# Dense products of the first layer as three fp32r products of split operands, in a new order of steps

## The chip, the core and the metric

The kernel runs on one core of a Trainium2 chip. Its time is the device time of one execution in microseconds (us). The engines of the core are called PE (matmul; PEld is its weight load), ACT (ScalarE), DVE (VectorE), POOL (GpSimd) and SP (SyncE, which only issues transfers).

## What is computed

Two transformer layers in fp32. The change concerns the first, a cross attention with a feed-forward network, over 8 batches. x and the context are stored channels first, 256 channels by 512 tokens each; there are 16 heads of 16 channels. Cut to what matters, the first layer is

```python
q  = transpose(zt_prev + pos_enc, (0, 2, 1));  kv = transpose(za + pos_enc, (0, 2, 1))
q  = layer_norm(q, ln_q_g, ln_q_b);            kv = layer_norm(kv, ln_kv_g, ln_kv_b)
Q, K, V = split(q @ Wq), split(kv @ Wk), split(kv @ Wv)
attn = einsum('bhqd,bhkd->bhqk', Q, K) / sqrt(DH)
ctx  = einsum('bhqk,bhkd->bhqd', softmax(attn), V)
r    = ctx @ Wo + q
h    = layer_norm(r, ffn_ln_g, ffn_ln_b)
out  = gelu(h @ W1 + b1) @ W2 + b2 + r         # W1: 256x512, W2: 512x256
```

The second layer takes this output (8 x 256 x 512): self attention, cross attention and a network of 512 to 2048 to 512. It is in the functions `attention_layer` (tiles "b_...") and the network behind it ("c_...").

## The kernel before

`first_layer` (tiles "a_...") runs one program per engine. Time is counted in iterations i = -2, -1, 0, ... of 16 positions; each position has two half positions. In iteration i the softmax of batch i runs, the tail (output product, normalising, network) of batch i-1, and the head (input, normalising, queries, keys) of batches i+1 and i+2. The last two iterations (7 and 8) are interleaved with the start of the second layer.

In each half position PE computes one exponent pair E (`exp_scores`, L461-472: two matmuls of 128x512 into `escore`) and one maximum pair M (`max_scores`, L475-484, into `mscore`, 9 positions ahead of E). ACT takes the exponent of E (L639, 128x1024, into a ring `pt`), DVE the row maxima of M (L802, `row_maximum`, 128x1024). E, ACT's exponent and M, DVE's maximum each have one buffer, so the next E or M waits for the engine behind it. The maxima of a group of four heads are turned ("m"), made negative and split (L646, L837), and go through DRAM into the rows of the operand `qst`.

Between these pairs PE does the filler that the table `STEPS` lists by position; in it ("f1", -1, 2, 0) is step f1 of batch i-1, tile m=2, contraction piece k=0:
- "pv" (L499): values weighed by the exponents, 16 matmuls of 32x512 a half position; "ctx" (L508) and "ctxT" (L516) turn the result to tokens (there DVE divides it by the row sum, `divide_context`) and to channels again;
- "y" (`output`, L522), "f1" (`up`, L569), "f2" (`down`, L577), "q" and "k" (`project`, L553) are fp32 products of 128x512, one a step: 4 y, 8 f1, 8 f2, 4 q, 4 k per batch; "v" (`values`, L561) is eight of 128x256;
- "tok" (L537) turns an input or the residual to tokens, where DVE normalises it (statistics L810-815, `apply` L822, with the reciprocal root on POOL, L446); "chan" (L546) turns it back, and ACT adds gain and shift (L691).

These fillers share four PSUM banks in the order of `STEPS`; `claim` waits for the reader of the use four before. ACT, DVE, SP and POOL follow orders of their own, written out in their functions `position` (L733, L873) and `body` (L404, L449). In position 8 ACT does `gelu` (L720), with a load of another function table before and behind it. `high_part` (ACT, L699) and `low_part` (DVE, L830) split queries and keys into two fp32r parts for the score matmuls: the high part is the value written as fp32r, the low part the value less the high part. SP writes these parts to DRAM (`put`) and reads them back stacked (`stack`, L384, per group of four heads). `fetch` brings the inputs of batch i+3, to which POOL adds the positions (L440).

## Time and profile before

| | us |
|---|---|
| time, median of 3 runs | 1841.54 (1839.46 to 1841.65) |
| time of the profiled execution | 1842.27 |
| span of the profiled execution | 1840.5 |
| PE busy in the span | 1717.6 (93%) |
| DVE busy | 1207.0 (66%) |
| ACT busy | 1060.4 (58%) |
| POOL busy | 142.4 (8%) |
| granted clock of PE, mean | 0.959 |

The first layer takes roughly the first 770 us of the span, the second the rest. The trace gives records: an instruction's start, its duration, and the idle time before it with what ended it. Matmuls are pipelined, so a record is longer than the distance to the next; distances from start to start tell the pace. One record of the trace is half of an fp32 128x512 product: its two passes are recorded each for itself.

### The profile page before, as it was taken

Reading aid. Unit: us, or ns where it says so; the run is one execution under the profiler, and the core shown is the slowest. Engines: PE = TensorE matmul, PEld = TensorE weight load, DVE = VectorE, ACT = ScalarE, POOL = GpSimd, SP = SyncE. Lnnn points to the kernel's source line nnn. Section 1 sums busy time; section 2 is a strip of 40 time slices with the busy share of each in tenths; the row PEclk is TensorE's granted clock in tenths of the full one; section 3 lists DMA queues with packets and bytes.
Section 4 is the critical chain, followed back from the end, with each engine's and each line's share of the span. In section 5 each row is a group of like instructions: output and inputs, shape, how many; then the busy total and the mean of one; then the engine's idle time right before and its main releaser. Section 6 shows DMA issues by size and latency. Waiting matters only on the chain.

```text
span 1840.5 us, 32546 instructions
## 1 busy us (share of the span) xinstructions
PE 1717.6 (93%) x11840; PEld 1233.4 (67%) x11840; DVE 1207.0 (66%) x2792; ACT 1060.4 (58%) x2333; POOL 142.4 (8%) x207
## 2 busy tenths in 40 slices
PE   3879999999999988999999999999999899999999
PEld 2424343444434333788889888888888789999998
DVE  5666776767776552588888888888888663333332
ACT  2345666756666564587788777777777631111111
POOL 2110101101000000000000000100000100000000
PEclk8779999999999898999999989999999999999999
DMA  6322223222222222567557757666666330000000
GB/s 161 111 86 67 94 82 100 71 93 88 83 71 68 80 61 87 152 157 182 153 156 200 198 163 200 169 173 173 167 167 168 116 121 25 25 25 25 25 26 13
DMA packets 169479, 201.62 MB, mean 110 GB/s; under 512 B 25956, under 2 KB 117220, under 8 KB 169320
## 3 DMA queue, kind: packets, MB, share of 16 engines
q1 hardware_dynamic: 169032, 199.14, 38.5%
q8 instruction: 95, 1.56, 0.4%
q10 hardware_dynamic: 288, 0.39, 0.2%
q14 instruction: 64, 0.52, 0.1%
HBM read 131.84 MB, written 67.63 MB: 108 GB/s over the span
## 4 chain that ended last, share of the span: by engine, by line
PE 81%; DVE 9%; ACT 5%; issue 2%; DVEq 1%; DMA 1%; ACTq 0%; POOL 0%; SPq 0%
PE c_d L2121 10%; PE b_d L1379 10%; PE c_sums L2136 10%; PE b_d L1391 9%; PE a_d L499 6%; PE b_d L1458 5%; PE a_escore L472 5%; PE a_d L569 3%; PE a_d L577 3%; PE a_mscore L484 3%; PE a_d L553 3%; PE b_score L1446 3%; PE b_d L1475 3%; DVE a_mx L802 2%; PE a_d L561 2%
## 5 line engine op out<-in xcount | busy, mean ns | idle before, releaser
L802 DVE TENSOR_REDUCE a_mx<-a_mscore 128x2 f32<-128x1024 f32 x247 | 302.3, 1224 | 171.8 <-PE a_mscore L484 170.2
L639 ACT ACTIVATE a_pt<-a_escore 128x1024 f32<-128x1024 f32 x256 | 262.5, 1025 | 165.1 <-PE a_escore L472 164.9
L1605 ACT ACTIVATE b_pr<-b_t,b_nmax 128x256 f32<-128x256 f32 x512 | 254.5, 501 | 121.4 <-DVE b_nmax L1781 121.0
L2220 ACT ACTIVATE c_gT<-c_d,c_b 128x256 f32<-128x256 f32 x128 | 53.7, 472 | 267.4 <-PE c_d L2121 267.4
L1777 DVE TENSOR_TENSOR b_t<-b_score,b_mask 128x1024 f32<-128x1024 f32 x128 | 155.0, 1211 | 75.6 <-PE b_score L1446 75.6
L1781 DVE CUSTOM_DVE_ANT_0 b_t<-b_t,b_minus 128x256 f32<-128x256 f32 x512 | 191.1, 429 | 16.9
L472 PEld LDWEIGHTS a_escore<-a_qst,a_kst 50*128 50x128 f32 x512 | 50.0, 191 | 180.4 <-ACT a_pt L639 109.6
L472 PE MATMUL a_escore<-a_qst,a_kst 50*128 50x512 f32 x512 | 133.8, 518 | 24.2 <-ACT a_pt L639 23.7
L2265 DVE CAST c_g_high<-c_gT 128x512 fp32r<-128x512 f32 x64 | 38.1, 595 | 172.0 <-ACT c_gT L2220 172.0
L2121 PE MATMUL c_d<-c_ln_high,c_w_high 128*128 128x256 f32 x512 | 145.4, 284 | 2.4 <-DVE c_ln_low L2267 2.4
L2121 PE MATMUL c_d<-c_ln_high,c_w_low 128*128 128x256 f32 x512 | 145.6, 284 | 0.0
L2121 PE MATMUL c_d<-c_ln_low,c_w_high 128*128 128x256 f32 x512 | 145.6, 284 | 0.0
L1458 PE MATMUL b_d<-b_ident,b_pr 128*128 128x128 f32 x1024 | 136.8, 277 | 4.9 <-DVE b_xr L1819 2.5
L1617 ACT ACTIVATE b_pt<-b_d 128x512 f32<-128x512 f32 x256 | 137.2, 590 | 4.5 <-PE b_d L1458 3.4
L484 PE MATMUL a_mscore<-a_kst,a_qst 48*128 48x512 f32 x494 | 113.0, 451 | 24.2 <-DVE a_mx L802 13.5
L499 PE MATMUL a_d<-a_pt,a_vaug 128*32 128x512 f32 x1024 | 131.2, 633 | 0.0
L1458 PEld LDWEIGHTS b_d<-b_ident,b_pr 128*128 128x128 f32 x1024 | 117.6, 143 | 6.1 <-DVE b_kparts L1752 3.1
L1379 PE MATMUL b_d<-b_lnp,b_wq 128*128 128x256 f32 x768 | 106.3, 298 | 15.5 <-DVE b_encp L1735 14.7
L1379 PEld LDWEIGHTS b_d<-b_lnp,b_wq 128*128 128x128 f32 x768 | 100.4, 203 | 18.6 <-issue 18.6
L2136 PE MATMUL c_sums<-c_w_high,c_g_high 128*128 128x512 f32 x256 | 102.0, 398 | 7.5 <-issue 6.7
L2121 PEld LDWEIGHTS c_d<-c_ln_high,c_w_high 128*128 128x128 f32 x512 | 98.8, 193 | 4.5 <-issue 2.6
L2136 PE MATMUL c_sums<-c_w_high,c_g_low 128*128 128x512 f32 x256 | 100.4, 392 | 0.0
(166 smaller groups left out, 3255.5 us busy)
## 6 DMA issues: line engine op xcount, KB each, us to landing
b_qst<-b_q SPq DMA_DIRECT2D x96, 256.0 KB, 4.7
b_kst<-b_k SPq DMA_DIRECT2D x96, 256.0 KB, 6.4
b_q<-b_qparts SPq DMA_DIRECT2D x64, 256.0 KB, 4.5
b_k<-b_kparts SPq DMA_DIRECT2D x64, 256.0 KB, 3.6
a_qst<-a_q_parts SPq DMA_DIRECT2D x192, 64.0 KB, 2.2
a_kst<-a_k_parts SPq DMA_DIRECT2D x186, 64.0 KB, 2.2
...
```

The costliest lines, as they stand in the source:

```text
L472: mm = nc.tensor.matmul(escore[:, e, :], kst[rows, pair, k * P:(k + 1) * P], qst[rows, pair, :], start=True, stop=True)
L484: mm = nc.tensor.matmul(maxima_bank(b, n)[:, e, :], qst[rows, pair, q * P:(q + 1) * P], kst[rows, pair, :], start=True, stop=True)
L499: mm = nc.tensor.matmul(at[32 * j:32 * j + 32, :], vaug[:, k, GROUP * g + j, :], pt[:, (b * UNITS + pair * TT + k) % RING, e, :], start=(k ...
L639: nc.scalar.activation(pt[:, at % RING, :, :], escore[:], ACT.Exp, scale=SCALE).then_inc(exp_done.sem, 1)
L802: nc.vector.tensor_reduce(mx[:, 2 * pair:2 * pair + 2, q], maxima_bank(b, n)[:], AX_X, ALU.max).then_inc(max_done.sem, 1)
L1379: mm = nc.tensor.matmul(at[:, j * S:(j + 1) * S], w[:, x, k, m:m + P], src[:, y, k, :], start=(k == 0 and c == 0), stop=(k == KT - 1 and c ...
L1391: mm = nc.tensor.matmul(at, src[:, x, k, n * P:(n + 1) * P], w[:, y, k, :], start=(k == 0 and c == 0 and not biased), stop=(k == KT - 1 an ...
L1458: last = nc.tensor.transpose(at[:, j * P:(j + 1) * P], pr[:, u % 2, j, k * P:(k + 1) * P], ident[:])
L1605: last = nc.scalar.activation(pr[:, u % 2, j, :], t[:, u % 2, j, :], ACT.Exp, scale=-1.0, bias=nmax[:, u, j:j + 1], accum_out=esum[:, u, j ...
L1781: last = nc.vector.tensor_tensor_reduce(t[:, u % 2, j, :], t[:, u % 2, j, :], minus[s][:, q, :], -1.0, HUGE, ALU.add, ALU.min, accum_out=n ...
L2121: mm = nc.tensor.matmul(bank[:, j * S:(j + 1) * S], w1[w][:, k, m:m + P], lnp[v][:, k, :], start=(k == 0 and n == 0), stop=(k == KT - 1 an ...
L2136: mm = nc.tensor.matmul(sums[:, t_, :], gp[v][:, u % RING, at:at + P], w2[:, row, :], start=(k == 0 and n == 0), stop=(k == FT - 1 and n = ...
```

## The change

All dense products of the first layer are made of three fp32r matmuls: high weights with high activations, high weights with low, low weights with high. The weights are loaded raw into the ring `pt`, and split once, by ACT (`high_weight`) and DVE (`low_weight`). The activations are split in every batch: the attention's context by ACT and DVE straight out of PSUM (`context`, `low_context`), queries and hidden by a copy on ACT (`high_queries`, `high_hidden`) and a subtraction on DVE (`low_queries`, `low_hidden`), gelu's output in two halves (`high_gelu`, `low_gelu`), the normalised key and value input on POOL (`split_context`: a cast and a subtraction). One tile `pair` holds the split context, hidden, low gelu half and queries in turn (`pair_free` waits for the last reader). Tiles are shared more: `xin` also holds the tokens and the turned input (`room`, `tokens_of`), `tokr` also the hidden. `STEPS` and the orders of ACT, DVE, POOL and SP are new.

```diff
-        wo = sb("wo", [P, CT, C])
+        wo = sb("wo", [P, 2, CT, C], F32R)
...
+        PRODUCTS = ((0, 0), (0, 1), (1, 0))
...
-            9: [("k", 1, 1, 0), ("k", 1, 1, 1), ("q", 1, 1, 0), "E0", "M0", ("q", 1, 1, 1), ("ctx", 0, 1), "E1", "M1", ("f2", -1, 0, 0)],
+            9: [("k", 1, 1, 0), ("k", 1, 1, 1), ("chan", 2, 1), ("f2", -1, 0, 0), ("f2", -1, 0, 1), ("f2", -1, 0, 2), ("f2", -1, 0, 3),
+                "E0", "M0", ("ctx", 0, 1), "E1", "M1", ("f2", -1, 1, 0), ("f2", -1, 1, 1)],
...
             def body(i):
-                put(i + 1, 0, 0)
                 stack(i, 3)
+                put(i + 1, 0, 1)
                 maxima(i, 1)
                 stack(i + 1, 0)
                 maxima(i, 2)
-                if i != -1:
-                    fetch(i + 3)
                 stack(i + 1, 1)
                 maxima(i, 3)
                 put(i + 1, 1, 1)
-                put(i + 1, 0, 1)
+                store(i - 1)
+                fetch(i + 3)
                 stack(i + 1, 2)
-                if i == -1:
-                    fetch(i + 3)
+                put(i + 2, 1, 0)
                 maxima(i + 1, 0)
-                store(i - 1)
-                put(i + 2, 1, 0)
+                put(i + 2, 0, 0)
...
+            def split_context(b):
...
+                nc.gpsimd.tensor_copy(kvp[b % 2][:, 0], room(b, 1)).then_inc(kvn_high.sem, 1)
+                kvn_high.need(pool, b, 1)
+                nc.gpsimd.tensor_tensor(kvp[b % 2][:, 1], room(b, 1), kvp[b % 2][:, 0].bitcast(F32), ALU.subtract).then_inc(kvn_low.sem, 1)
...
+            def products(at, w, src, steps, k):
+
+                for n, (x, y) in enumerate(PRODUCTS):
+                    mm = nc.tensor.matmul(at, w(x), src(y), start=(k == 0 and n == 0), stop=(k == steps - 1 and n == 2))
+                return mm
...
             def up(b, m, k):
-                pe_.wait_ge(chan_done[2].sem, chan_done[2].at(b, k + 1))
+                if b == 0 and m == 0 and k == 0:
+                    w_low.need(pe_, 0, 5)
+                h_low.need(pe_, b, 1)
                 at = claim(pe_, "f1", b, m) if k == 0 else bank("f1", b, m)
-                mm = nc.tensor.matmul(at, w1[:, k, m * P:(m + 1) * P], hT[:, k, :], start=(k == 0), stop=(k == CT - 1))
+                mm = products(at, lambda x: w1[:, x, k, m * P:(m + 1) * P], lambda y: pair[:, y, k, :], CT, k)
...
+            def high_weight(n):
...
+                nc.scalar.activation(WEIGHTS[n][1][:, 0], staged(n), ACT.Copy).then_inc(w_high.sem, 1)
...
+            def high_queries(b):
...
+                nc.scalar.activation(pair[:, 0], qnT[b % 3][:], ACT.Copy).then_inc(qn_high.sem, 1)
...
             def gelu(b):
...
-                act.wait_ge(f1_raw.sem, f1_raw.at(b, FT))
-                nc.scalar.activation(gT[:], gT[:], ACT.Gelu).then_inc(g_done.sem, 1)
+                for h in range(2):
+                    act.wait_ge(f1_raw.sem, f1_raw.at(b, 2 * h + 2))
+                    nc.scalar.activation(gT[:, 2 * h:2 * h + 2, :], gT[:, 2 * h:2 * h + 2, :], ACT.Gelu).then_inc(g_done.sem, 1)
...
+                nc.scalar.activation(gh[:, 2 * h:2 * h + 2, :], gT[:, 2 * h:2 * h + 2, :], ACT.Copy).then_inc(g_high.sem, 1)
...
+                nc.vector.tensor_tensor(pair[:, 1], qnT[b % 3][:], pair[:, 0].bitcast(F32), ALU.subtract).then_inc(qn_low.sem, 1)
```

In the second layer the split of its first two weights moves from positions 8 and 10 (DVE 9 and 11) to 8 and 12 (9 and 13) of iteration 7, its second weight is loaded later, and two waits are added, on ACT for the last sum of batch 6 (`summed`), on DVE for `free_weighed`.

What stands in a row on PE, from E of position 8's second half to position 10, before (`a_kvnT`, `a_qnT` are the normalised inputs, `a_gT` gelu's output, one row is one or more code steps, 4 transposes are "ctx", 8 are "chan" or "tok"):

```order
L499 MATMUL a_d<-a_pt,a_vaug 32x512 x8
L553 MATMUL a_d<-a_kvnT,a_wk 128x512 x2
L553 MATMUL a_d<-a_qnT,a_wq 128x512
L472 MATMUL a_escore<-a_qst,a_kst 128x512 x2
L484 MATMUL a_mscore<-a_kst,a_qst 128x512 x2
L553 MATMUL a_d<-a_qnT,a_wq 128x512
L508 MATMUL a_d<-a_ident,a_ctxr 128x128 x4
L472 MATMUL a_escore<-a_qst,a_kst 128x512 x2
L484 MATMUL a_mscore<-a_kst,a_qst 128x512 x2
L577 MATMUL a_d<-a_gT,a_w 128x512
```

and now (`a_kvp` is the split key input, `a_xin` the key tokens, `a_gh` and `a_pair` gelu's high and low part, each product three rows' worth):

```order
L605 MATMUL a_d<-a_kvp,a_wk 128x512 x6
L637 MATMUL a_d<-a_ident,a_xin 128x128 x8
L605 MATMUL a_d<-a_gh,a_w 128x512
L605 MATMUL a_d<-a_pair,a_w 128x512
L605 MATMUL a_d<-a_gh,a_w 128x512 x2
L605 MATMUL a_d<-a_pair,a_w 128x512
L605 MATMUL a_d<-a_gh,a_w 128x512 x2
L605 MATMUL a_d<-a_pair,a_w 128x512
L605 MATMUL a_d<-a_gh,a_w 128x512 x2
L605 MATMUL a_d<-a_pair,a_w 128x512
L605 MATMUL a_d<-a_gh,a_w 128x512
L555 MATMUL a_escore<-a_qst,a_kst 128x512 x2
```

The channel turn and the first four W2 products now stand ahead of E(9,0), and the query products are gone from there.

PE, positions 13 to 15 (second half of 12 to the next E of position 0), before:

```order
L508 MATMUL a_d<-a_ident,a_ctxr 128x128 x4
L546 MATMUL a_d<-a_ident,a_tokn 128x128 x8
L472 MATMUL a_escore<-a_qst,a_kst 128x512 x2
L484 MATMUL a_mscore<-a_kst,a_qst 128x512 x2
L553 MATMUL a_d<-a_kvnT,a_wk 128x512
L472 MATMUL a_escore<-a_qst,a_kst 128x512 x2
L484 MATMUL a_mscore<-a_kst,a_qst 128x512 x2
L553 MATMUL a_d<-a_kvnT,a_wk 128x512
L472 MATMUL a_escore<-a_qst,a_kst 128x512 x2
L484 MATMUL a_mscore<-a_kst,a_qst 128x512 x2
L553 MATMUL a_d<-a_qnT,a_wq 128x512
L472 MATMUL a_escore<-a_qst,a_kst 128x512 x2
```

and now:

```order
L591 MATMUL a_d<-a_ident,a_ctxr 128x128 x4
L555 MATMUL a_escore<-a_qst,a_kst 128x512 x2
L567 MATMUL a_mscore<-a_kst,a_qst 128x512 x2
L605 MATMUL a_d<-a_pair,a_wq 128x512 x3
L555 MATMUL a_escore<-a_qst,a_kst 128x512 x2
L567 MATMUL a_mscore<-a_kst,a_qst 128x512 x2
L605 MATMUL a_d<-a_pair,a_wq 128x512 x3
L555 MATMUL a_escore<-a_qst,a_kst 128x512 x2
L567 MATMUL a_mscore<-a_kst,a_qst 128x512 x2
L605 MATMUL a_d<-a_pair,a_wq 128x512 x3
L555 MATMUL a_escore<-a_qst,a_kst 128x512 x2
L567 MATMUL a_mscore<-a_kst,a_qst 128x512 x2
```

The turns have left for positions 8 and 11, and one query product of three matmuls stands behind each M but the last.

ACT around gelu (position 8), before (`a_mparts` is the negative maxima, `a_ctxr` the context):

```order
L639 ACTIVATE a_pt<-a_escore 128x1024
L646 ACTIVATE a_mparts<-a_d 16x128
L720 ACT_TABLE_LOAD
L720 ACTIVATE a_gT<-a_gT 128x2048
L639 ACT_TABLE_LOAD
L639 ACTIVATE a_pt<-a_escore 128x1024
L656 ACTIVATE a_ctxr<-a_d 128x512
L639 ACTIVATE a_pt<-a_escore 128x1024
```

and now:

```order
L740 ACTIVATE a_pt<-a_escore 128x1024
L747 ACTIVATE a_mparts<-a_d 16x128
L842 ACTIVATE a_gT<-a_d,a_b 128x512
L849 ACT_TABLE_LOAD
L849 ACTIVATE a_gT<-a_gT 128x1024 x2
L856 ACTIVATE a_gh<-a_gT 128x1024
L757 ACTIVATE a_ctxr<-a_d 128x512
L856 ACTIVATE a_gh<-a_gT 128x1024
L740 ACT_TABLE_LOAD
L740 ACTIVATE a_pt<-a_escore 128x1024
L827 ACTIVATE a_kparts<-a_d 128x512
```

The exponent of position 8's second half comes behind the two gelu halves, the two copies, and a context copy.

## Rows read from the trace of the kernel before

**Rows 1.** the page's first part, PE's line: busy time, share, instructions

```profile
PE 1717.6 (93%) x11840; PEld 1233.4 (67%) x11840; DVE 1207.0 (66%) x2792; ACT 1060.4 (58%) x2333; POOL 142.4 (8%) x207
```

**Rows 2.** busy time by window: stretch, length, each engine's busy us, granted clock, DMA

```profile
396.69:476.74 80.05, 78.47 (x405) 33.84 (x404) 56.57 (x92) 52.41 (x67) 7.74 (x5) 1.00 0.28 88
```

**Rows 3.** timeline of PE: start, us, line, operation, form, count [idle before <-releaser]

```profile
400.19 1.92 PE L499 MATMUL a_d<-a_pt,a_vaug 128*32 128x512 f32 x16
...
402.04 0.51 PE L472 MATMUL a_escore<-a_qst,a_kst 50*128 50x512 f32 x2
...
408.39 1.04 PE L516 MATMUL a_d<-a_ident,a_ctxt 128*128 128x128 f32 x8
...
409.36 0.50 PE L472 MATMUL a_escore<-a_qst,a_kst 50*128 50x512 f32 x2
...
410.02 1.98 PE L522 MATMUL a_d<-a_ctxT,a_wo 128*128 128x512 f32 x4
...
411.94 0.51 PE L472 MATMUL a_escore<-a_qst,a_kst 50*128 50x512 f32 x2
...
427.97 1.55 PE L569 MATMUL a_d<-a_hT,a_w 128*128 128x512 f32 x3 [0.73 <-ACT a_hT L691]
```

**Rows 4.** timeline of PE and of DVE around one maximum pair

```profile
452.56 0.44 PE L484 MATMUL a_mscore<-a_kst,a_qst 48*128 48x512 f32 x2
...
453.05 1.23 DVE L802 TENSOR_REDUCE a_mx<-a_mscore 128x2 f32<-128x1024 f32 x1 [0.60 <-PE a_mscore L484]
...
454.42 0.50 PE L484 MATMUL a_mscore<-a_kst,a_qst 48*128 48x512 f32 x2
```

**Rows 5.** timeline of PE in the second layer, fp32r records

```profile
1500.65 0.40 PE L2136 MATMUL c_sums<-c_w_high,c_g_high 128*128 128x512 f32 x1
...
1500.88 0.40 PE L2136 MATMUL c_sums<-c_w_rest,c_g_high 128*128 128x512 f32 x1
```

**Rows 6.** groups by line and form: busy us, mean ns of one | idle before

```profile
L822 DVE TENSOR_SCALAR a_tokn<-a_tokn,a_mv,a_rstd 128x256 f32<-128x256 f32 x96 | 33.0, 404 | 2.3 <-POOL a_rstd L446 2.3
...
L440 POOL TENSOR_TENSOR a_xin<-a_xin,a_pe 128x1024 f32<-128x1024 f32 x14 | 32.8, 2364 | 32.5 <-DMA a_xin<-in_x 25.0 <-DVE a_tokn L822 7.5
...
L1728 DVE TENSOR_TENSOR b_lnp<-b_lnT,b_lnp 128x1024 fp32r<-128x1024 f32 x16 | 19.5, 1222 | 18.5 <-ACT b_lnp L1554 18.5
...
L1554 ACT ACTIVATE b_lnp<-b_lnT 128x1024 fp32r<-128x1024 f32 x16 | 17.1, 1066 | 0.1
...
L1338 POOL MEMSET b_bo<- 128x1024 f32 x1 | 1.0, 951 | 25.2 <-DMA hidden<-a_outT 25.2
```

**Rows 7.** timeline of DVE around statistics and of ACT around gelu

```profile
419.02 1.39 DVE L810 BATCH_NORM_STATS2 a_stats<-a_tokn 128x6 f32<-128x256 f32 x4
...
421.02 1.22 DVE L802 TENSOR_REDUCE a_mx<-a_mscore 128x2 f32<-128x1024 f32 x1
...
439.27 0.25 ACT L646 ACTIVATE a_mparts<-a_d 16x128 fp32r<-16x128 f32 x1
...
444.06 1.02 ACT L639 ACTIVATE a_pt<-a_escore 128x1024 f32<-128x1024 f32 x1
```

**Rows 8.** timeline: the start on DVE, SP and PE

```profile
26.09 0.69 DVE L830 TENSOR_TENSOR a_qparts<-a_d,a_qparts 128x512 fp32r<-128x512 f32 x1 [1.03 <-ACT a_qparts L699]
...
29.58 5.45 SPq L384 DMA_DIRECT2D a_qst<-a_q_parts  x12
...
38.03 0.80 PE L484 MATMUL a_mscore<-a_kst,a_qst 48*128 48x512 f32 x2 [10.54 <-DMA a_kst<-a_k_parts]
...
73.20 0.49 PE L472 MATMUL a_escore<-a_qst,a_kst 50*128 50x512 f32 x2 [0.36 <-DVE a_mx L802]
```

**Rows 9.** busy time by window, as rows 2

```profile
556.78:713.95 157.17, 141.42 (x683) 56.53 (x682) 83.20 (x118) 96.54 (x115) 2.81 (x4) 0.92 0.24 68
...
623.80:627.20 3.40, 2.07 (x14) 1.13 (x12) 2.62 (x3) 2.10 (x3) 0.00 (x0) 1.00 0.42 161
...
627.20:640.90 13.70, 11.44 (x39) 3.58 (x39) 6.55 (x6) 5.38 (x6) 0.00 (x0) 0.50 0.22 58
```

414 lines of the change are left out of this document (281 added, 133 removed), and 22 rows, old and new, of the table STEPS.

## The prediction

> **What bounds the kernel now.** First the page: TensorE (PE) is busy for 93% of the span [rows 1]. That averages two different layers, so I read single batches of the first layer, from their first score matmul E to the next batch's: it takes 80.05 us, PE busy 78.5, VectorE (DVE) 56.6, ScalarE (ACT) 52.4, at full clock [rows 2]. PE is the bound, almost without a gap. The batch has 32 half positions, each with an exponent pair E, a maximum pair M and some filler. From start to start E and M take 0.66 together (409.36 to 410.02), sixteen records of weighing values 1.85, eight transposes 0.97, and four records of dense work 1.92 [rows 3]. Those four records are two matmuls of the code: one fp32 128x512 product costs 0.96 us. The PE column of a batch is therefore 21.4 (32 of E and M, at 0.67), 14.8 (8 of values), 8.7 (72 transposes), 0.8 (maxima turned), 26.9 (28 products) and 3.8 (V, 8 half as wide): 76.4, and 3.6 us of waits, the largest of them 0.73 at the first W1 product [rows 3].
>
> Behind PE stands a loop that no filler shortens: M, then its row maximum on DVE, then the next M, since M has one bank pair. M at 452.56, reduce at 453.05, next M at 454.42: 1.86 us [rows 4]; I take 1.83. A half position whose filler is under 1.83 - 0.67 = 1.16 us gains nothing from cheaper filler.
>
> **Part 1, three split products for one.** A 128x512 record of fp32r is followed by the next after 0.23 [rows 5]. A dense product becomes 3 x 0.23 = 0.69 in place of 0.96, and V's of 128x256, half as wide, 0.36 in place of 0.48. Per batch 28 x 0.27 + 8 x 0.12 = 8.5 us less PE, 68.0 left.
>
> **Part 2, the splitting.** Per batch ACT gets four copies of 128x1024 (queries, hidden, two gelu halves) at 1.07 [rows 6], about 0.94 from start to start: 3.8 us, and ACT goes to 56. DVE gets four subtractions of 128x1024 at 1.22 [rows 6] and two of 128x512 at 0.69 [rows 8], about 1.14 and 0.60 from start to start: 5.8 us, and DVE goes to 62. GpSimd (POOL) gets the context's split: a subtraction, priced like the add at 2.36, and a cast that no row has. Its bounds are 0.95 (a fill of 128x1024) and 2.36 (that add, with two inputs) [rows 6]; I take 1.6, halfway, since it reads one input and writes one output. Once the loop runs, the first key step comes over 6 us after the context's tile is turned, so either end costs nothing there; in the start it is on the path.
>
> **Part 3, the new order, walked through 32 half positions.** For each I took the latest of three: PE's filler plus 0.67; the 1.83 loop; and DVE's reduce (1.14) plus what stands between two reduces: statistics 2.00 (419.02 to 421.02 [rows 7]), applying 1.3 (four at 0.40, overlapping [rows 6]), a division 0.68, a residual or output sum 0.65 (near the 0.69 of [rows 8]). The same walk over the order before gives 79.7 where the trace has 80.05; I use differences. For the new order it gives 77.1: 67.7 of PE and 9.4 of waits:
> - 13.0 to 0.0, 4.1 us. One query product per half position makes 0.67 + 0.69 = 1.36, which the loop stretches to 1.83 four times (1.9); 15.1 has no filler at all (1.2); at 13.0 the low half of the queries, 1.14 on DVE, holds the reduce (1.0).
> - 9.0 to 11.1, 2.5 us: six reduces, two output sums, a division and an apply keep DVE busy for 10.2, and PE has 9.6.
> - 5.0 to 6.1, 2.0 us: the channel turn waits for statistics and apply (0.8), the first W1 product for ACT's added copy and DVE's subtraction (0.9).
> - 3.1 and 8.1, 0.8 us. ACT's gelu block (maxima, table load, gelu, table load, from 439.27 to 444.06: 4.8 [rows 7]) gets two copies (1.9), a context copy (0.5) and the last W1 copy (0.5) into it: 7.7. PE has 7.6 of filler there (values, keys, a channel turn, four W2 products), so the block is hidden but for 0.5.
>
> A batch saves 79.7 - 77.1 = 2.55 us of the 8.5. This holds for batches 0 to 5: 6 x 2.55 = **15.3**.
>
> **Part 4, batches 6 and 7.** There the steps for batch b+2 are absent: no keys and no channel turn beside gelu, no queries later. From 556.78 to 713.95, E of batch 6 to the last E, the two took 157.2 us, at a mean clock of 0.92 [rows 9]; the walk at full clock gives 76.5 + 71.6 = 148.1, so some 9 us of it are half clock, in three stretches, the longest 627.20 to 640.90 [rows 9]. After the change the walk gives 75.6 + 71.6 at full clock: **0.9** saved, as what the products give is lost to the 7.7 us of gelu block that nothing covers: without keys and turn PE has 4.6 us of filler there (values 1.85, four W2 products 2.76) for 7.7. Such a hole of 3 us leaves PE busy for less than in the stretch before 627.20 (2.07 of 3.40), after which the clock fell. Three stretches cost 9, so one costs about 3; one or two more are likely. I take **+4**, ends 0 and +8.
>
> **Part 5, the start.** Before, the queries' low half starts at 26.09 and takes 0.69, the first stacking is issued at 29.58, the first M runs at 38.03 and the first E at 73.20 [rows 8]. The change lengthens this chain. Context cast and subtraction on POOL: 1.6 + 2.4, less 0.6 that PE needed for its first products anyway, 3.4. The queries' copy on ACT and the subtraction on DVE: 2.2. SyncE (SP) now stacks after both halves of the queries: 0.8 to 1.5. That is 6.4 to 7.1 to the first M. Between first M and first E, 35.2 us, DVE takes 18 maxima, statistics and applies in turn, and gets two low halves of queries at 1.1 more: +2 to +4 with the waits they shift. I take **+9**, ends +4 (the splits overlap) and +13 (cast at 2.36, nothing overlaps). The six weight splits sit in the idle 10.54 us before the first M [rows 8].
>
> **Part 6, edits at nothing.** SP's queue: a stacking of twelve issues takes 5.45 us [rows 8], and in the walk each group still lands over 4 us before its M. The shared pair buffer: each user comes two or more positions after the last reader. Reusing the input tiles delays the fetch to position 11; its adds are due 8 positions later. The added waits of the second layer are for events some 15 us old. In the tail 20 products give back 5.4 us of PE, and six splits on ACT and DVE take about as much on the last batch's chain: 0, ends -4 and +4.
>
> **The sum.** 1842.3 (the profiled run, 0.8 above the median 1841.5 of three) + 9 - 15.3 - 0.9 + 4 + 0 = **1839**.
>
> **Rivals.**
> A. More of the gain comes. DVE's loop has slack that the walk doesn't see, and a batch saves 5 to 8.5 us: at 5, 1839 - 6 x 2.45 = 1824; all of it, 1803. Against it stands the 1.86 between two Ms [rows 4]. 0.13.
> B. POOL and DVE in each other's way, the slower case. The queries' low half (both inputs in SBUF) runs at 12.1 to 13.0, about when POOL, with the late fetch, adds positions to two tiles, 2 x 2.36 [rows 6]. No row has a two-input DVE operation beside a POOL one. If one waits for the other, it costs 0.7 (the rest of one add) to 4 us, where every M already waits for DVE, in the six iterations that fetch. From 1.1 us each it makes the kernel slower than 1845; at 2.1 it is 1839 + 13 = 1852. 0.14.
> The Trainium skill (SBUF — State Buffer, section "Who interferes with whom") states such a rule: a DVE instruction of this kind and a GpSimd one that reads SBUF exclude each other, and the second to start is held for the whole of the first. By it rival B holds; no row here shows it yet.
> C. The clock in every batch. One stretch with PE busy 2.07 of 3.40 us was followed by half clock [rows 9]; in the new order 14.1 to 15.1 has PE records over about 2.3 of 3.4. If the clock falls there, the PE-bound work of positions 0 and 1 runs at half pace: +1.7 to +3.4 in each of batches 0 to 5, 1839 + 6 x 2.5 = 1854. 0.18.
> The Trainium skill (TensorE: Matmul & The Clock Gate, section "HAM oscillation — how this bites in real kernels") warns of this, idle gaps inside a kernel that throw the clock back; by it the sum would be rival C's.
> D. The split doesn't pay per product: between short records of changing weights 0.27 in place of 0.23. The loops hide half: 1839 + 6 x 1.7 = 1849. 0.05.
>
> **How the numbers follow.** Forecast 0.50 (1830 to 1848, as start and clock term move), A 0.13, B 0.14, C 0.18, D 0.05. A measurement here can tell about 0.2%, 3.7 us, from no change. Faster than 1837.8: 0.23 of the forecast, A's 0.13, 0.02 each of B and C: 0.40. Within 0.2%: 0.17 of the forecast, 0.02 of B, 0.02 of C: 0.21. Slower: 0.39. The forecast lies inside the 0.2%, but its own width spreads it to both sides. The range leaves out half of A and the far ends of B and C: 1820 to 1859.
>
> **What would show it.** Right: batches 0 to 5 at 77 to 78 us and batch 6 hardly shorter than 77.5; M waiting for DVE at 13.1 to 15.1 with 1.8 us from E to E; fp32r records 0.23 apart; first E at 80 to 84. B shows as a queries' subtraction over 1.22 or a POOL add over 2.36. C shows as a granted clock of 0.5 inside batches 1 to 5. Wrong if 8.1 takes over 9 us in a full batch, or if a batch is under 75.

## The result

The changed kernel takes 1890.96 us (median of 4 runs, 1890.81 to 1893.02), the kernel before 1841.07 beside it: the ratio is 1.0271, 95% interval 1.0256 to 1.0286. The forecast was 1839 with a range up to 1859; the change is slower by 50 us. The profiled execution spans 1889.1 us, 48.6 more than before. The table says where they went, by the start of the first E of each batch. All tables and distances here come from one profiled execution of each kernel.

| stretch | before | after | difference | forecast |
|---|---|---|---|---|
| up to the first E | 73.2 | 82.0 | +8.8 | +9 |
| batches 0 to 5 | 483.6 | 490.9 | +7.3 | -15.3 |
| batches 6 and 7 | 157.2 | 170.0 | +12.9 | +3.1 |
| behind the last E | 1126.5 | 1146.1 | +19.6 | 0 |

The page of the changed kernel, PE's busy line (compare [rows 1]) and the granted clock in 40 slices:

```profile
PE 1708.0 (90%) x12128; PEld 1290.6 (68%) x12128; DVE 1260.4 (67%) x2846; ACT 1095.5 (58%) x2379; POOL 171.5 (9%) x223
...
PEclk9679999999998897889999999999999899999999
```

PE is busy for 10 us less, in a span 49 us longer. Counted from 0, the clock's digits in slices 12 to 17, the end of the first layer and the hand-over to the second, are 7 to 9, and in slices 1 and 2 they are 6 and 7. Busy time by window, columns as in [rows 2] (the granted clock is the third from the end), for batches 2, 3, 6 and 7:

```profile
245.88:329.34 83.46, 77.12 (x440) 40.66 (x441) 63.66 (x98) 56.56 (x73) 12.13 (x7) 0.96 0.30 86
329.34:410.15 80.81, 76.12 (x440) 40.34 (x441) 62.04 (x98) 56.46 (x73) 12.19 (x7) 0.98 0.29 85
572.92:657.41 84.49, 74.58 (x390) 35.65 (x391) 53.09 (x69) 50.22 (x61) 1.01 (x1) 0.87 0.22 65
657.41:742.96 85.55, 66.77 (x346) 32.26 (x346) 38.79 (x59) 51.86 (x61) 1.80 (x3) 0.84 0.22 61
```

Against [rows 2] DVE has 62.0 in batch 3 (forecast 62), ACT 56.5 (forecast 56), so the added work was sized right. But no full batch is shorter than 80.7, where 77 to 78 was forecast; batch 2 takes 83.5 at a clock of 0.96. Batches 6 and 7 have clocks of 0.87 and 0.84, together 0.92 before [rows 9].

From here on "8.1" is the second half of position 8, and what it "takes" is the time from its E to the next E.

**The price of a product.** The timeline of PE before, inside the four records that [rows 3] show in one line, from 410.02 to the E at 411.94. The second and the third record start at

```profile
410.56 1.02 PE L522 MATMUL a_d<-a_ctxT,a_wo 128*128 128x512 f32 x2
...
410.99 1.02 PE L522 MATMUL a_d<-a_ctxT,a_wo 128*128 128x512 f32 x2
```

From the second on, a record follows after 0.43, so one fp32 product, two records, costs 0.86. The step from the first to the second is 0.11 longer and the step from the last to E 0.09. After the change, two products (six records) in the same place:

```profile
342.07 0.50 PE L605 MATMUL a_d<-a_pair,a_wo 128*128 128x512 f32 x1
...
342.40 0.63 PE L605 MATMUL a_d<-a_pair,a_wo 128*128 128x512 f32 x2
...
343.10 0.63 PE L605 MATMUL a_d<-a_pair,a_wo 128*128 128x512 f32 x2
...
343.33 0.39 PE L605 MATMUL a_d<-a_pair,a_wo 128*128 128x512 f32 x1
...
343.65 0.50 PE L555 MATMUL a_escore<-a_qst,a_kst 50*128 50x512 f32 x2
```

0.33 for the first, then 0.23 each (0.70 from 342.40 to 343.10 for three), and 0.32 from the last to E. Three fp32r matmuls cost 0.70, and the same 0.2 is paid again for each run of products, that is for each stretch of them between two score matmuls: from the first record to E it is 1.58 in place of 1.92. A product saves 0.16, not 0.27.

**The hand-over.** The last batch's network beside the second layer: ACT's hidden copy, DVE's low half, the first W1 product; then ACT's last copy of values, its last W1 copy, DVE's low gelu, the first W2 product.

```profile
778.35 1.06 ACT L817 ACTIVATE a_pair<-a_tokn 128x1024 fp32r<-128x1024 f32 x1
...
781.68 1.23 DVE L995 TENSOR_TENSOR a_pair<-a_tokn,a_pair 128x1024 fp32r<-128x1024 f32 x1
...
782.96 0.80 PE L605 MATMUL a_d<-a_pair,a_w 128*128 128x512 f32 x1 [6.18 <-DVE a_pair L995]
...
796.72 0.60 ACT L1775 ACTIVATE b_val<-b_d 128x512 f32<-128x512 f32 x1 [2.12 <-PE b_d L1582]
...
797.21 0.68 ACT L842 ACTIVATE a_gT<-a_d,a_b 128x512 f32<-128x512 f32 x1
...
810.00 2.35 DVE L1009 TENSOR_TENSOR a_pair<-a_gT,a_gh 128x1024 fp32r<-128x1024 f32 x2
...
811.28 0.79 PE L605 MATMUL a_d<-a_gh,a_w 128*128 128x512 f32 x1 [12.77 <-DVE a_pair L1009]
```

The hidden copy ends at 779.4, the subtraction starts at 781.68, behind the second layer's normalising on DVE. PE has finished W1 by 791.2, but the last W1 copy stands behind two value copies in ACT's order and starts at 797.21. Gelu's low half stands on DVE behind a subtraction and a softmax step of the second layer and starts at 810.00, though the copy it needs was there at 803.1. PE waits for 6.2 and 12.8 us.

### The profile page after: what moved, and what is told of

It is laid out like the page before. It is cut to its first block, busy times and chain, and to the rows that moved or that the text cites. A ratio compares the mean times of both kernels' runs of the same rounds, so it can differ in the third digit from the quotient of the medians.

```text
span 1889.1 us, 33291 instructions
## 1 busy us (share of the span) xinstructions
PE 1708.0 (90%) x12128; PEld 1290.6 (68%) x12128; DVE 1260.4 (67%) x2846; ACT 1095.5 (58%) x2379; POOL 171.5 (9%) x223
## 4 chain that ended last, share of the span: by engine, by line
PE 74%; DVE 15%; ACT 6%; issue 3%; DVEq 1%; DMA 1%; POOL 0%; SPq 0%; ACTq 0%
PE a_d L605 11%; PE c_d L2314 10%; PE c_sums L2329 9%; PE b_d L1570 9%; PE b_d L1582 8%; PE a_d L582 5%; PE a_escore L555 5%; PE b_d L1649 4%; DVE a_mx L947 4%; PE a_mscore L567 3%; PE b_score L1637 3%; PE b_d L1666 2%; ACT a_pt L740 2%; DVE b_t L1973 2%; DVE b_t L1969 2%
## 5 line engine op out<-in xcount | busy, mean ns | idle before, releaser
L582 PE MATMUL a_d<-a_pt,a_vaug 128*32 128x512 f32 x1024 | 135.5, 651 | 0.0
L567 PE MATMUL a_mscore<-a_kst,a_qst 48*128 48x512 f32 x494 | 115.7, 462 | 21.4 <-DVE a_mx L947 15.3
```

Of the source, the lines that this page charges most:

```text
L582: mm = nc.tensor.matmul(at[32 * j:32 * j + 32, :], vaug[:, k, GROUP * g + j, :], pt[:, (b * UNITS + pair * TT + k) % RING, e, :], start=(k ...
```

## The experiments

Unless it says otherwise a run is set against the changed kernel, and times are medians; full batches are those of batches 1 to 5 without a fall of the clock. Sixteen kernels ran, and all of them are told of here.

### The hand-over in another order

```diff
             for p in range(4, 8):
                 ahead(TAIL, p)
+            ahead(TAIL, 8)
             value(0, 0)
             value(0, 1)
-            ahead(TAIL, 8)
```

on ACT, and on DVE positions 5 to 7 ahead of `normalise(1)`, and 8 ahead of `turned_low(1)` and `soften(0, 0)`.

> The changed kernel with one edit at the hand-over to the second layer (iteration 8): ACT does position 8 (copy of the last W1 tile, gelu, its high parts) ahead of two value copies of the second layer, DVE does positions 5 to 8 (low hidden, low gelu) ahead of the second layer's normalising, its low part and its first softmax step. Theory, order: in the changed kernel PE waits 6.2 us before W1 and 12.8 us before W2 of the last batch; some 2 us of the first, 6 of the second (last W1 copy behind the value copies) and 6 more (low gelu half behind softmax of the second layer) are only order. W2 then starts near 797 in place of 811, and the time falls from 1891 by 11 to 16, to 1875 to 1880. Rival, the split itself (its copies and subtractions on the last batch's chain, at half clock) makes the loss behind the last E: the time falls by under 3.

Measured: 1874.95, 16 less, at the upper end; behind the last E 1128.9 in place of 1146.1. DVE's low gelu and the first W2 product:

```profile
797.41 2.36 DVE L1009 TENSOR_TENSOR a_pair<-a_gT,a_gh 128x1024 fp32r<-128x1024 f32 x2 [8.57 <-ACT a_gh L856]
...
800.25 0.40 PE L605 MATMUL a_d<-a_gh,a_w 128*128 128x512 f32 x1
```

The W2 product starts at 800 where 797 was expected, in an execution whose last E is 3.5 us later (746.4 in place of 743.0). Of the 19.6 us behind the last E 17.2 were the order of these positions on ACT and DVE; 2.4 stay.

### POOL against DVE, and the clock

The two position adds on POOL and the low half of the queries on DVE in batch 2 of the changed kernel, and the M behind them:

```profile
313.69 5.67 POOL L513 TENSOR_TENSOR a_xin<-a_xin,a_pe 128x1024 f32<-128x1024 f32 x2 [10.45 <-DMA a_xin<-in_x]
...
314.66 2.49 DVE L1001 TENSOR_TENSOR a_pair<-a_qnT,a_pair 128x1024 fp32r<-128x1024 f32 x1
...
318.34 0.49 PE L567 MATMUL a_mscore<-a_kst,a_qst 48*128 48x512 f32 x2 [1.34 <-DVE a_mx L947]
```

The subtraction takes 2.49 where its like takes 1.22 [rows 6], and the two adds 5.67 where two take 4.7. In batch 3 the subtraction came first and took 1.20, and the second add 3.35; in batch 5, where no add runs beside it, it took 1.20. In these rows whichever starts second is late by about what is left of the first. The Trainium skill (SBUF — State Buffer, section "Who interferes with whom") states that such a pair excludes each other; by that rule this is what must come, and these rows agree.

```diff
+                qn_low.need(pool, b - 1, 1)
                 for s in range(2):
                     pool.wait_ge(x_in[s].sem, x_in[s].at(b, 1))
```

> The changed kernel with one edit: POOL starts the two position adds of a batch only after DVE has written the low half of the queries. Theory B (POOL and DVE hold each other): the low half of the queries, 2.09, 2.49 and 1.98 us in batches 1, 2 and 4 (1.20 in 3, 5), takes 1.20 in all; the half position 13.1 of these batches goes from 2.77, 3.15, 2.65 to 1.87, and the time falls by 3 to 4 us; by 5 to 8 if the falls of the clock right behind these holes go with them. Rival, the falls of the clock come first and make the half positions long: under 1 us.

Measured: 1891.67, no difference in the median (the profiled execution, 1886.58, was the fastest of the four). The mechanism is as the theory said, and the time isn't: it is the rival's, though not for the rival's reason. The low half takes 1.20 in all batches,

```profile
313.99 1.20 DVE L1002 TENSOR_TENSOR a_pair<-a_qnT,a_pair 128x1024 fp32r<-128x1024 f32 x1
```

and 13.1 is 1.85 to 1.89 everywhere; the falls of the clock behind it are gone. But 0.0, 2.8 when nothing disturbs it, now takes 4.3 to 4.7 us in batches 1, 2, 4 and 5, where in the changed kernel only batches 1 and 6 had 4.5 and more: the clock goes to half there instead, behind 15.1, which has no filler. Idle work on PE against that:

```diff
+            IDLE_WORK = {(13, 1): 1, (14, 0): 1, (14, 1): 1, (15, 0): 1, (15, 1): 4}
...
+                for _ in range(IDLE_WORK.get((p, j), 0)):
+                    nc.tensor.matmul(bank("m", i + 1, 1), wk[:, 0, 0, 0:P], wq[:, 0].rearrange("p k n -> p (k n)"), start=True, stop=True)
```

> The changed kernel with idle work added on PE, whose results nobody reads: one fp32r product of 128x512 more in half positions 13.1, 14.0, 14.1 and 15.0, four in 15.1, in iterations 0 to 5 (48 in all, some 11 us of PE work). Theory C (the clock falls for lack of work and costs time): the granted clock stays at 1 in batches 1 to 5, where it fell near 236, 321, 389, 484 and 552, and the time falls by 4 to 8 although work is added. Rival (these half positions are held by the maximum loop and the clock costs nothing there): the time stays within 1 or grows by up to 2.

Measured: 1897.05, 6 us more. Both sides missed: the clock still falls behind POOL's hole at 13.1, and at half clock the added records are on the path: PE is then busy without a gap. In batch 3 the four half positions 13.1 to 15.0 took 4.1 and three times 3.15. The window of a stretch there, columns as in [rows 2], has a clock of 0.50:

```profile
401.40:404.80 3.40, 3.40 (x12) 1.66 (x8) 1.23 (x1) 1.12 (x2) 0.00 (x0) 0.50 0.00 0
```

All three edits (hand-over, POOL, idle work):

> The three edits together: the order at the hand-over, POOL's adds behind the low half of the queries, and the idle work on PE. If the causes are separate the gains add up: 1891 less 18 to 24 is 1867 to 1873, still slower than before, as a full batch stays at about 80.8 and the start and batches 6 and 7 are as they were. Rival (POOL's holes are what lets the clock fall, one cause, counted twice): 1871 to 1877.

Measured: 1866.08, ratio to the kernel before 1.0139 (1.0124 to 1.0154). That is 0.9 below the range of the sum. Against the hand-over alone it is 8.9 less, where POOL's edit alone gave nothing and the idle work alone lost 6. The two only work together, so neither of the two accounts, sum or one cause, is right as put. Batch 4:

```profile
407.87:487.55 79.68, 75.84 (x449) 40.93 (x448) 62.22 (x98) 56.45 (x73) 11.19 (x7) 1.00 0.29 88
```

A full batch at full clock takes 79.7, and 80.05 before: 0.4 us of the forecast 2.55. The idle work itself is on the path in 13.1 (2.10 in place of 1.87) and 15.1 (1.82 in place of 1.77); without it a batch that nothing disturbs would take some 79.4, an estimate, and save 0.65.

Batch 3 of this kernel still takes 82.6: the clock is at half from 385.0 to 391.8, in 11.0 and 11.1, behind 9.0 to 10.1. The changed kernel has the same in batches 3 and 5. This is neither rival B nor rival C.

### What a full batch waits for

These three leave parts of the computation out, as their expectations say; they start from the kernel with the three edits, and each ran once (1854.58, 1880.08 and 1832.52 us). What is read from them is the length of their batches.

```diff
-                nc.vector.tensor_tensor(pair[:, 1], hT, pair[:, 0].bitcast(F32), ALU.subtract).then_inc(h_low.sem, 1)
+                nc.vector.tensor_tensor(pair[:, 1, :, 0:8], hT[:, :, 0:8], pair[:, 0, :, 0:8].bitcast(F32), ALU.subtract).then_inc(h_low.sem, 1)
```

and alike for context, queries and gelu.

> The kernel with the three edits (order at the hand-over, POOL behind the low queries, idle work), with DVE's low halves of context, hidden, gelu and queries cut to 8 columns; the product of high weight and low activation takes the high activation again, so low activations are left out of the result and PE's work is the same. Theory (DVE's subtractions sit between maxima only in places): a full batch goes from 79.7 to 78.4. Rival (DVE's 4.6 us are all on the path): to 75.

```profile
162.54:240.83 78.29, 75.33 (x449) 41.02 (x449) 56.98 (x98) 56.39 (x73) 11.21 (x7) 1.00 0.30 90
```

78.3: of 5.2 us less on DVE (57.0 in place of 62.2) 1.4 were on the path, as the theory said. Next, fp32 again:

```diff
-                for n, (x, y) in enumerate(PRODUCTS):
-                    mm = nc.tensor.matmul(at, w(x), src(y), start=(k == 0 and n == 0), stop=(k == steps - 1 and n == 2))
-                return mm
+                return nc.tensor.matmul(at, w(0).bitcast(F32), src(0).bitcast(F32), start=(k == 0), stop=(k == steps - 1))
```

> The run before this one with one fp32 product of the high parts in place of the three fp32r products (low parts of weights and activations left out). This measures the disputed price. Theory now: from record to record an fp32 product costs 0.86 and three fp32r 0.70, and 0.2 more per run of products in either form, so a product in place saves 0.16: a full batch is 3.5 to 4.5 us longer than in the run before this one, 82 to 83. As predicted (0.27 saved per product): 6.5 to 7.5 us longer, 85 to 86.

```profile
412.52:495.02 82.50, 80.02 (x413) 35.46 (x413) 57.13 (x98) 56.45 (x73) 11.13 (x7) 1.00 0.28 85
```

82.5, 4.2 more: the price of 0.16 per product holds, and 0.27 falls. The half position 2.1 (two products) went from 2.26 to 2.58.

The batch of 82.5 says something else too. It has fp32 products as the kernel before, but the new order and ACT's copies, and nearly nothing of DVE's low halves, and it takes 2.45 us more than the 80.05 before (part of it the idle work). So the account of a batch is: new order and copies +2.45, three fp32r matmuls for one fp32 -4.2, DVE's low halves +1.4, together -0.4. The new order costs more than half of what the products give; no run has the split products in the order of before.

The last of the three has `w(0), src(0)` without the bitcasts.

> The same with one fp32r product of the high parts alone (all low parts left out of the result), which takes 0.47 us per 128x512 product and 14.9 us per batch from PE. If PE were the bound everywhere, a full batch would go from 78.4 to 63.5. Theory (the maximum loop of 1.83 and ACT and DVE take over in some 20 half positions): to 73.5 to 75.

```profile
389.33:467.45 78.12, 70.03 (x377) 31.90 (x376) 56.73 (x98) 56.24 (x72) 11.12 (x7) 0.89 0.31 90
```

78.1 to 78.5, and 82.3 to 82.5 in two batches: much the same as the 78.3 with three products. The expectation of 73.5 to 75 missed, since the clock falls in each batch (0.89 here). In batch 4 it is at half from 436.5 to 453.6, and there 11.0 and 12.0 take 3.7 and 4.8 us where they took 2.8 and 2.7 with three products. Not all is the clock: 8.0 takes 4.1 for 2.7 at full clock, as its M waits for a maximum on DVE. In full batches taking this work from PE gives nothing back. The kernel as a whole is 22 us shorter than with three products, 8.0 up to the first E, 10.6 in batches 6 and 7 and 7.0 behind the last E, while batches 0 to 5 take 3.4 more.

### Iterations 6 and 7

ACT around gelu in batch 6 of the changed kernel, and PE beside it (the keys of batch 7, and the first W2 product):

```profile
618.19 1.28 ACT L849 ACT_TABLE_LOAD   x1
...
625.17 1.03 ACT L740 ACTIVATE a_pt<-a_escore 128x1024 f32<-128x1024 f32 x1
...
621.09 1.67 PE L605 MATMUL a_d<-a_kvp,a_wk 128*128 128x512 f32 x6
...
623.82 0.50 PE L605 MATMUL a_d<-a_gh,a_w 128*128 128x512 f32 x1 [1.07 <-DVE a_pair L1009]
```

From table load to the next exponent it is 7.0 us; PE's filler in front of W2 ends at 622.8 and W2 waits for the low half. 8.1 took 8.3 us in batch 6 (5.3 before), as in a full batch, and 10.0 in batch 7 (5.0 before). But the kernel before has its W2 products behind 8.1, and what 8.1 takes more the positions behind it give back: 8.1 to 11.1 together are 19.2 and 20.5 us in batches 6 and 7, and were 19.0 and 21.0.

What is left of the loss lies elsewhere. The new table has in 5.1 and 6.0 the tokens of batch b+2 alone, and in 11.0 and 11.1 its channel turn and keys; the table before has W2 products in 11.0 and 11.1. Iterations 6 and 7 have no batch b+2, so PE has only E and M there. Windows of 11.0 and 11.1 and of 12.0 in batch 6, then from E of 8.1 to the first W2 product, and from there to E, in batch 7:

```profile
634.28:637.73 3.45, 1.99 (x11) 0.81 (x10) 2.77 (x4) 2.05 (x2) 0.00 (x0) 1.00 0.00 0
637.73:643.11 5.38, 5.13 (x22) 1.16 (x22) 1.94 (x2) 1.29 (x2) 0.00 (x0) 0.53 0.65 197
703.97:709.46 5.49, 2.36 (x23) 0.60 (x19) 1.23 (x1) 5.48 (x6) 0.00 (x0) 1.00 0.02 6
709.46:714.00 4.54, 4.54 (x13) 3.31 (x13) 1.23 (x1) 4.24 (x5) 0.00 (x0) 0.62 0.00 0
```

12.0 to 13.0 take 3.4 and 4.5 us more than before in the two batches, 6.1 to 7.1 take 3.0 and 3.6 more. In the two batches the clock is at half in eight stretches, some 50 us together, where the kernel before has three, some 25 us. (The mean clocks say the same: 2 x 0.13 x 84.5 + 2 x 0.16 x 85.6 = 49, and 2 x 0.08 x 157.2 = 25.) Only one of the eight, from 709.75 to 713.16, lies at gelu.

```diff
+        LATE_STEPS = {
+            9: [("k", 1, 1, 0), ("k", 1, 1, 1), "E0", "M0", ("ctx", 0, 1), "E1", "M1", ("f2", -1, 0, 0), ("f2", -1, 0, 1)],
+            10: ["E0", "M0", ("f2", -1, 0, 2), ("f2", -1, 0, 3), "E1", "M1", ("f2", -1, 1, 0)],
+            11: ["E0", "M0", ("f2", -1, 1, 1), ("f2", -1, 1, 2), "E1", "M1", ("f2", -1, 1, 3)],
+        }
```

with ACT's `high_gelu`, DVE's `low_gelu` and `network_out` behind the exponents and maxima they stood ahead of, and the weight splits of the second layer moved, as the expectation says.

> The kernel with the three edits, and an order of its own for iterations 6 and 7, in which keys and a channel turn are no longer there to cover gelu: the exponent of 8.1 comes right behind gelu, the copies of gelu's output and DVE's subtractions follow one by one, W2 products stand in positions 9 to 11, and the second layer's first two weights are split at positions 10 and 13 of iteration 7 in place of 8 and 12. Theory (the longer gelu block without cover and the clock falls that follow from it make +5.3 and +5.9 in batches 6 and 7): batch 6 from 82.8 to 80, batch 7 from 85.5 to 82, time from 1866 to 1858 to 1862. Rival (the loss there is half clock from other holes, at 5.0 to 6.1 and 12.0): under 2 us.

Measured: 1860.17, 5.9 less than with the three edits; batch 6 is 80.1 as expected, batch 7 83.6 where 82 was. The time is the theory's, the place is not. 8.1 is back at 5.3 and 5.5, but 8.1 to 11.1 together are 0.9 and 0.1 longer than with the three edits; the gain is in 12.0 to 13.0, 3.4 and 4.5 shorter, where the clock no longer falls behind 11.1, as W2 products now stand there. So the holes that the rival named, not gelu's length, made that part of the loss, and the rival's "under 2 us" had them too small. The one at 5.1 and 6.0 is as it was. Batch 6:

```profile
564.54:644.61 80.07, 70.00 (x392) 35.07 (x391) 52.65 (x69) 49.73 (x61) 1.01 (x1) 0.92 0.23 68
```

Then two edits at once, of the order of PE's steps in position 5 and of DVE's normalising step:

```diff
-            5: ["E0", "M0", ("chan", -1, 2), ("ctx", 0, 0), "E1", "M1", ("tok", 2, 0)],
+            5: ["E0", "M0", ("ctx", 0, 0), ("chan", -1, 2), "E1", "M1", ("tok", 2, 0)],
...
                 if p == 10:
-                    if i > FIRST:
-                        apply(i + 2, 0)
...
                 if p == 8:
+                    if i > FIRST:
+                        apply(i + 2, 0)
```

> The kernel with the three edits and the late order, with two edits more: DVE applies the query tokens' normalising in position 8, while it waits for gelu's copies, in place of position 10 between two maxima; and PE turns the context's first group ahead of the channel turn in 5.0. Theory (DVE, not PE, holds 9.0 to 11.0: it is free for some 5 us beside gelu and full behind it): the half position 11.0 goes from 3.0 to about 2.0, 5.0 from 2.9 to 2.5, a full batch from 79.7 to 78.3, the clock falls in 11.0 of batches 0 and 3 go (5 to 6 us together), and the time from 1860 to 1845 to 1850. Rival (PE or ACT is next at once): a full batch over 79.2 and the time over 1855.

Measured: 1861.44, 1.3 more than the run before it, a miss. 11.0 went to 2.05 and 5.0 to 2.44 as expected; but 8.1 went from 8.3 to 9.0, and 5.1 from 2.1 to 3.3. So the first hunk, that of position 5, was taken back:

> The kernel with the three edits, the late order and the earlier apply alone, with 5.0 as the change has it (channel turn ahead of the context's first group). Theory (the edit in 5.0 spoiled the last step: 5.1 went from 2.1 to 3.3): 5.0 and 5.1 are back at 2.9 to 3.1 and 2.1, 11.0 stays near 2.05, 8.1 near 8.3, a full batch 78.7 to 79.0. Rival (the earlier apply itself costs as much in 8.1, 8.3 to 9.0, as it gives in 11.0): a full batch 79.4 to 79.7.

Measured: 1852.13, from one run. 5.1 is back at 2.08, 8.1 stays at 8.94, and a full batch takes 79.4: the rival held. What DVE does in position 8 ahead of the low gelu halves delays W2 by 0.7 of the 1.0 that position 11 gains. It did take the fall of the clock in 11.0 out of batch 3 (82.6 to 79.4). Batch 4:

```profile
399.97:479.41 79.44, 75.81 (x449) 40.98 (x448) 61.78 (x98) 56.46 (x73) 11.17 (x7) 1.00 0.29 89
```

Idle work at the end of iterations 6 and 7, on top of the two edits:

```diff
+                if late(i) and p >= 14:
+                    at = claim(pe_, "m", i + 1, 1) if there(i + 1) else claim(pe_, "pv", i, 3)
+                    for _ in range(4):
+                        nc.tensor.matmul(at, w1[:, 0, 0, 0:P], w2[:, 0, 0:2].rearrange("p k n -> p (k n)"), start=True, stop=True)
```

> The kernel before it with idle work on PE in the last two positions of iterations 6 and 7 as well: four fp32r products of 128x512 in each of the half positions 14.0 to 15.1, which have only E and M there. Theory (these stretches, not gelu, let the clock fall into 0.0 of batch 7 and behind the last E): 0.0 of batch 7 goes from 5.6 to 2.8, the stretch behind the last E gets shorter by 2, and the time falls by 4 to 6. Rival: within 2.

Measured: 1857.25, 4.2 less than with the two edits. 0.0 of batch 7 is 2.76, the stretch behind the last E 2.3 shorter.

### The start

The changed kernel: POOL's cast and subtraction, DVE's low queries, PE's first key products, first query products, first M and first E ([rows 8] has the last two of before).

```profile
21.12 1.04 POOL L527 CAST a_kvp<-a_gT 128x1024 fp32r<-128x1024 f32 x1 [3.53 <-ACT a_gT L802]
...
22.24 2.35 POOL L529 TENSOR_TENSOR a_kvp<-a_gT,a_kvp 128x1024 fp32r<-128x1024 f32 x1
...
28.85 1.45 DVE L1001 TENSOR_TENSOR a_pair<-a_qnT,a_pair 128x1024 fp32r<-128x1024 f32 x1
...
24.64 2.93 PE L605 MATMUL a_d<-a_kvp,a_wk 128*128 128x512 f32 x6 [3.36 <-POOL a_kvp L529]
...
30.35 1.22 PE L605 MATMUL a_d<-a_pair,a_wq 128*128 128x512 f32 x2 [2.78 <-DVE a_pair L1001]
...
42.48 0.79 PE L567 MATMUL a_mscore<-a_kst,a_qst 48*128 48x512 f32 x2 [5.38 <-DMA a_qst<-a_q_parts]
...
81.99 0.80 PE L555 MATMUL a_escore<-a_qst,a_kst 50*128 50x512 f32 x2 [1.82 <-DVE a_mx L947]
```

The cast takes 1.04 (1.6 was taken), the low queries stand behind the keys' low half and again beside a POOL add, 1.45 in place of 1.22.

```diff
-                if not there(b):
+                if not there(b) or b == 0:
...
+                        nc.vector.tensor_copy(kvp[0][:, 0], room(0, 1)).then_inc(kvn_high.sem, 1)
+                        kvn_high.need(dve, 0, 1)
+                        nc.vector.tensor_tensor(kvp[0][:, 1], room(0, 1), kvp[0][:, 0].bitcast(F32), ALU.subtract).then_inc(kvn_low.sem, 1)
+                        low_queries(0)
```

> The kernel before it with another start: DVE splits the context of batch 0 (a copy and a subtraction, 1.8 us) in place of POOL (1.04 and 2.35), and writes the low half of its first queries before it waits for the first keys' high part, in place of behind it. Theory (the start's loss is this chain): the first query products move from 30.4 to about 26.5, the first M from 42.5 to 38.5 or 39, the first E by 3 to 4, and the time falls by 3 to 4. Rival (DMAs or the half clock hold the first E): first M earlier, first E within 1.

Measured: 1854.03, 3.2 less than the run before it, with its six times spread from 1849.4 to 1860.6. The time alone would not show the gain; the profile does: first query product at 25.8, first M at 38.85, first E at 76.1, 5.0 earlier. The chain is the cause, and about half of the start's loss can be had back.

And all of it together, with 40 transposes that nobody needs ahead of the first M, where PE waits for the transfers of the first queries and keys; the edit of position 5 is left out.

```diff
+                if (i, p) == (FIRST + 1, 7):
+                    for _ in range(40):
+                        nc.tensor.transpose(mscore[:, 0, 0:P], ident[:], ident[:])
```

> That kernel with idle work at the end of iterations 6 and 7, the other start (DVE splits the first context, the low queries ahead), and 40 transposes of the identity on PE ahead of the first M, where PE waits for DMAs. It is the best form of the change that these runs point to. Theory: 1854 less 6 (full batches and their clock falls) less 2 to 4 (the first positions at full clock): 1844 to 1848, not faster than before the change. Rival (the split pays once its holes are closed): under 1837.

Measured: 1850.26, ratio 1.0052 (1.0038 to 1.0066), a miss by 2.3 us: 1844 to 1848 was expected. The first E is at 78.4, 2.3 later than without the 40 transposes, so they show no gain: the clock stayed at 1 up to 38.7 only, and the first M came at 39.9. Full batches take 79.4, batch 7 still 82.9. The best form of the change found here is still 0.5% slower than the kernel before.

### The kernel before with idle work

```diff
+                if LAST - 2 <= i < LAST and p >= 14:
+                    at = claim(pe_, "m", i + 1, 1) if there(i + 1) else claim(pe_, "pv", i, 3)
+                    for _ in range(8):
+                        nc.tensor.transpose(at[:, 0:P], ident[:], ident[:])
```

> The kernel before the change with idle work alone: eight 128x128 transposes of the identity on PE in each half position 14.0 to 15.1 of iterations 6 and 7. Theory (part of what batches 6 and 7 take is half clock, 627 to 641 and 709 to 719): 0.0 of batch 7 goes from 5.8 to 2.9, and the time from 1841 by 4 to 6, to 1835 to 1837, though work is added. Rival (the clock falls anyway, from other holes): within 1.

Measured: 1836.48 against 1840.23, ratio 0.9981 (0.9973 to 0.9990), 3.8 us less, just short of the 4 expected. From E to E at 0.0 of batch 7, the kernel before, and then this one:

```profile
634.31:640.09 5.78, 5.40 (x22) 1.26 (x23) 2.34 (x2) 1.29 (x2) 0.00 (x0) 0.50 0.47 128
```

```profile
632.28:635.14 2.86, 2.86 (x22) 0.88 (x21) 1.54 (x2) 1.17 (x2) 0.00 (x0) 1.00 0.47 135
```

5.78 at half clock became 2.86 at full. It is faster than the changed kernel and 0.2% faster than the kernel before, with work added.

On top of that, 88 transposes ahead of the first M, in the place and the form of the last diff above.

> The kernel before the change with the idle work in iterations 6 and 7 and 88 transposes of the identity on PE ahead of the first M, where PE waits for DMAs for 10.5 us and the clock then is at half up to the first E (mean 0.63). Theory (PE's work there is longer for it): first E from 73.2 to 68 to 70, time from 1836.5 to 1832 to 1834. Rival (DVE's 18 maxima hold this stretch): first E within 1 of 70 to 73, time within 1.5.

Measured: 1837.91, ratio 0.9985; the first E is at 73.1 (73.2 in the kernel before; 70.1 in the last run, which differs from it only behind this stretch, so a first E moves by 3 us by itself). The rival's numbers held, but the test did not part the two: the clock was at 1 up to the first M at 38.1 and at half from 40.1 on. From 48.8 to 60.4 DVE was busy without a gap, from there to the first E PE was, for 12.3 of 12.7 us at a clock of 0.59. That DVE's maxima pace the whole stretch is not shown.

And on top of those, work behind the second half of position 8 of iteration 7:

```diff
+                if i == LAST - 1 and p == 8 and j:
+                    at = claim(pe_, "ctx", i, 1)
+                    for _ in range(16):
+                        nc.tensor.transpose(at[:, 0:P], ident[:], ident[:])
```

> The run before this one with 16 transposes more on PE in 8.1 of iteration 7, where it waits some 2.5 us for the gelu block. Theory: the fall of the clock into 9.0 to 10.0 of batch 7 (3.3, 2.7 and 4.1 us) goes, these three half positions take 6.5 us together in place of 10, and the time falls by 2 to 3 more. Rival (they wait for ACT's weight copies, not for the clock): within 1.

Measured: 1837.63, ratio 0.9983. 9.0, 9.1 and 10.0 of batch 7 take 3.3, 2.7 and 4.1 as before it. The rival's number held again, and its reason for 9.0 alone: the clock is at 1 up to 683.7, and the E at 684.02 waits 2.15 for the exponent that ACT took at 682.94, behind two copies of second-layer weights. Through 9.1 and 10.0 PE is busy for 6.84 of 6.84 us at a clock of 0.53, so these two are half clock after all, which the added transposes did not keep away.

## Why the prediction was wrong

**Right, partly by luck: the start** (+9, measured +8.8). Its two parts were off in opposite ways: 4.5 to the first M where 6.4 to 7.1 stood, and 4.3 behind it where 2 to 4 stood. Right too: the loads of ACT and DVE, the M loop (13.1 to 15.0 at 1.83 when nothing disturbed them), 8.1 of a full batch (8.3; under 9 had been put as the test), and rival B's mechanism.

**Wrong, part 1, the term 28 x 0.27 + 8 x 0.12 = 8.5.** It took the mean of a run of four records [rows 3] as the price of one, and set it against the distance inside a long run of fp32r records [rows 5]. Each run of products pays 0.2 in either form. Counted so it is (28 + 4) x 0.16 = 5.1, and the run with fp32 products measured 4.2 of it on the path. My walk with 0.86, 0.70 and 0.2 per run, an estimate, gives 80.0 for the order before (the trace 80.05) and 79.3 for the new one, with 11.0 at 2.5 and 5.1 at 1.7 where the trace has 3.0 and 2.1; so it must be some 0.5 too long in others. A batch saves 0.4, some 0.65 without the idle work, so 15.3 becomes 2 to 4. (The walk as put had small slips too: 5.0 to 6.1 stands at 2.0 where its parts add up to 1.7, and 76.4 less 8.5 is 67.9, not 67.7.)

**Wrong, part 3, rivals as exclusive cases.** The forecast held if neither B nor C came; both came, and each hid the other. With the three edits batches 0 to 5 took 7.4 us less (483.5 for 490.9), and 11.3 less than in the profile of the hand-over run (494.8), which has the same first layer as the changed kernel; so much do the falls of the clock vary. B was priced at 0.7 to 4 us a batch and took 0.8 to 1.3 in three. C was priced at 2.5 in six batches; behind B's holes, in 14.0 to 15.0, it took 1.0, 2.4 and 1.0, and without one 1.9 in 0.0 of batch 1. A third place that no rival named, 11.0 and 11.1 behind the W2 products, took 1.4 and 1.7 in batches 3 and 5. Rivals with one consequence should have been added, not weighed apart.

**Wrong, part 4, the hole: +12.9 for +3.1.** It looked for PE's idle time beside gelu alone and took one or two more stretches of half clock at 3 us each. There were five more, eight for three, and only one at gelu. The others lie behind positions that the new table leaves to batch b+2, 5.1, 6.0, 11.0 and 11.1, and at the end of the iteration; that gelu's block grew by itself changed 8.1 to 11.1 by +0.2 and -0.5 us. For the one at gelu in batch 7 the mechanism was as put: PE was busy for 2.36 of 5.49 us, and the next 4.54 had a clock of 0.62. The Trainium skill (TensorE: Matmul & The Clock Gate, section "HAM oscillation — how this bites in real kernels") says that such gaps bring the clock down inside a kernel, and these rows agree.

**Wrong, part 6, the tail at 0, ends -4 and +4.** It summed PE's gain against the splits' durations and didn't walk the queues. The hand-over interleaves the positions of iteration 8 with steps of the second layer as the kernel before did; but the change moves the last W1 copy from position 7 to 8 on ACT and puts the low gelu half into position 8 on DVE, and so both stand behind steps of the second layer. That was 17.2 us, the largest single miss.

In sum the forecast was 52 us off: some 11 to 13 from the price of a product, 9 to 11 from POOL and the clock in batches 0 to 5, 10 from iterations 6 and 7, 20 from the hand-over.

**Open.** Why DVE's order at position 8 keeps a full batch at 79.4. Whether the split products in the order of the kernel before, or in another one, would let more of the 4.2 us through: no run tried it, and it is the obvious next one. What keeps the clock at half up to the first E.
